# The low 64 columns of B: from ten split passes over the whole array to four full passes on its halves

## The chip, the cores and the metric

The kernel runs on one core of a Trainium2 chip. The metric is the device time of one execution in microseconds. The engines of the core are TensorE (PE, with its weight loads shown apart as PEld), VectorE (DVE), ScalarE (ACT), GpSimd (POOL) and SyncE (SP), each with its own stream of instructions, held in step by semaphores.

## The reference, cut to what matters

A small language-model tower over 32 sequences of 256 tokens and width D = 192: four gated recurrent layers, then one attention block and one quantised feed-forward block. The change touches one product in the layers:

```
def _block(x, g, bt, Wi, bi, cw, cb, wd, bd_, wB, bB_, wC, bC_, wo, bo):
    h = _layernorm(x, g, bt)
    uv = h @ Wi.T + bi
    u, v = (uv[..., :D], uv[..., D:])
    uc = _dwconv_causal(u, cw, cb)
    delta = jax.nn.softplus(uc @ wd.T + bd_)
    Bm = uc @ wB.T + bB_
    Cm = uc @ wC.T + bC_
    y = _selective_scan(uc, delta, Bm, Cm)     # decay exp(-delta), input uc * Bm, output sum(h * Cm)
    y = y * jax.nn.sigmoid(v)
    return x + (y @ wo.T + bo)
for l in range(4):
    x = _block(x, ...)
```

## The kernel before, in words

The rows of x stay in SBUF. In the layers the work is cut into items: one item is two sequences (2 x 256 tokens) of one layer, so 16 items a layer and 64 in all. Activations lie with the features on the partitions: the high 128 of the 192 features on 128 partitions (`uc_h`, both sequences side by side, 512 columns), the low 64 features of sequence 0 on partitions 0 to 63 and of sequence 1 on partitions 64 to 127 (`uc_l`, 256 columns).

Most products run on fp32r operands, which TensorE takes in one pass but which are rounded. To keep fp32 accuracy, the rows and the weights are split into a rounded part and a rest: ACT rounds `uc` into `ucr_h` and `ucr_l` (round_uc, L1031), DVE subtracts (rest_of_uc, L1299) into `ucr_r` and into the other half of `ucr_l`. ACT rounds the layer's weights `raw_z` into `w_z` (round_weights, L947) and DVE writes `w_z_rest` (split_weights, L1220). A product of 128 output columns is then five passes of 512 columns (z_product, L589). B's low 64 output columns are made by b_low_product (L598): for each of the two sequences five passes of 256 columns, and in each pass a 128-wide slice of `w_z` of which one half is zeros (`B_LOW`, the padding of `Z_COLS`), so that sequence 0 lands on PSUM partitions 0 to 63 of bank B_BL and sequence 1 on partitions 64 to 127. That is 10 of the passes of an item; the others of the z and C family are 20 of 512 columns, and uv_product has 15.

A product on plain fp32 operands shows in the trace as two records for each matmul instruction, one on fp32r as one. Plain fp32 is used in rows (L651): `w_o` with `sv_h` (L676, 128 rows of the array), and `w_o` with `sv_l` (L683) on the two halves of the array's rows, tile by tile in turn, half b writing bank `B_O[b]`. In the attention phase, values (L763) places four heads on the four quarters of the array's columns (L775); all four write one bank.

Each engine's order is written out by hand: steps (L254) runs one software-pipelined step for each item. On PE a step is uv of one item, z_c of the item before it, transposes, rows of the item two back, then b_c: z_product for B's high columns (bank B_BH), b_low_product (B_BL), z_product for C's (B_CH). b_c ends with semaphores `b_done` and `c_done`; DVE's recurrence (L1313) waits for them. Four early steps of layers 0, 1 and 2 (each layer's items 2 to 5) also carry the preparation of the next layer's weights: means (L566) on PE, centre_weights and split_weights on DVE, round_weights on ACT. The steps of the first layer carry DVE's place (L1230), which adds the position rows to the gathered embeddings.

Of the kernel before, what the change touches and what calls it, by code (L numbers as in the profile page):

```python
# [7 lines left out]
F32 = mybir.dt.float32  # L8
# [4 lines left out]
ACT = mybir.ActivationFunctionType  # L13
AX = mybir.AxisListType.X

P = 128
D = 192
HI, LO = 128, 64
S = 256
# [4 lines left out]

UV_H, UV_L, UV_V, UV_COLS = 0, 128, 256, 384

Z_H, Z_LC, B_PAD, B_H, C_H, Z_COLS = 0, 128, 256, 448, 576, 704

B_LOW = (B_PAD + 64, B_PAD)
EPS = 1e-5  # L30
H, DH = 12, 16
R = 4
# [4 lines left out]
F32R = mybir.dt.float32r  # L37
# [3 lines left out]
def wait(eng, sem, value):  # L41

    if isinstance(value, int) and value <= 0:
        return
    eng.wait_ge(sem, value)


def build(nc, tokens, embedding, pos_enc, w_uv_d, w_z_d, w_o_d, gain_d, vec_d, bout, w_qkv_d, b_qkv_d, w_out_d,
# [9 lines left out]
    with ExitStack() as ctx:  # L58
# [6 lines left out]
        def sem(name):  # L65
            return ctx.enter_context(nc.semaphore(name))
# [30 lines left out]
        def sa(name, shape, dt=F32):  # L97
            return layers_memory.enter_context(nc.sbuf_tensor(name, shape, dt))
# [4 lines left out]
        raw_z = sa("raw_z", [P, 2, Z_COLS])  # L103
# [3 lines left out]

        xs = sa("xs", [P, CT, 2 * D], F32R)
        ht = [sa(f"ht_{k}", [P, 2 * S], F32R) for k in range(3)]
        w_z = sa("w_z", [P, 2, 2, Z_COLS], F32R)  # L110
        w_z_rest = sa("w_z_rest", [P, 2, 2, Z_COLS], F32R)
        ucr_h = sa("ucr_h", [P, 2, 2 * S], F32R)

        ucr_l = sa("ucr_l", [P, 2, 2 * S], F32R)
        ucr_r = sa("ucr_r", [P, 2, 2 * S], F32R)
        w_o = sa("w_o", [P, L, 2, D])

        stats = sa("stats", [P, CT, 6])
        mv = sa("mv", [P, CT, 2])
# [6 lines left out]
        uc_h = sa("uc_h", [P, 2, 2, S])  # L126
        uc_l = sa("uc_l", [P, 2, S])
# [70 lines left out]
        w_rounded = sem("w_rounded")  # L198
# [48 lines left out]
        def half(b):  # L247

            return slice(b * LO, (b + 1) * LO)
# [309 lines left out]
        def _(pe):  # L559
# [38 lines left out]
            def b_low_product(l, s, out):  # L598


                for b in range(2):
                    c, w_s, q = slice(B_LOW[b], B_LOW[b] + HI), l % 2, slice(b * S, (b + 1) * S)
                    passes = ((w_z[:, w_s, 0, c], ucr_h), (w_z[:, w_s, 1, c], ucr_l), (w_z[:, w_s, 0, c], ucr_r),
                              (w_z_rest[:, w_s, 0, c], ucr_h), (w_z_rest[:, w_s, 1, c], ucr_l))
                    for k, (w, r) in enumerate(passes):
                        last = nc.tensor.matmul(out[:, 0:S], w, r[:, s, q], start=(b == 0 and k == 0),  # L606
                                                stop=(b == 1 and k == len(passes) - 1))
                return last

            def uv(it, centred):  # L610
# [79 lines left out]
            def b_c(it):  # L690
                if it is None:
                    return
                n, l, c, s = it
                wait(pe, ht_ready, ahead(n, 3))
                z_product(l, B_H, s, B_BH)
                b_low_product(l, s, B_BL).then_inc(b_done, 1)
                z_product(l, C_H, s, B_CH).then_inc(c_done, 1)
# [242 lines left out]
        def _(act):  # L940
# [6 lines left out]
            def round_weights(l):  # L947
                s = l % 2
                wait(act, c_done, (l - 1) * NCH)
                act.wait_ge(s_layer[l], W_LAYER)  # L950
                for k in range(2):
                    act.activation(w_z[:, s, k, :], raw_z[:, k, :], ACT.Identity).then_inc(w_rounded, 1)
                act.wait_ge(w_centred, 3 * (l + 1))
                for k in range(3):
                    act.activation(w_uv[:, s, k, :], raw_uv[:, k, :], ACT.Identity).then_inc(w_rounded, 1)
# [88 lines left out]
            def gates(it):  # L1044
# [9 lines left out]
                act.activation(sv_h[:, s, :], B_VH[:], ACT.Sigmoid, bias=v(l, 0, V_BV)).then_inc(sv_ready, 1)  # L1054

            round_weights(0)

            def turned(src, dst, t_sem, n, done):
# [58 lines left out]
            def step(at, l, k):  # L1117
                save_u(at(2), 1)
                first_tap(at(2), 1)
                save_u(at(2), 0)  # L1120
                first_tap(at(2), 0)
                decay(at(3))
                save_turned(at(1))
                round_rows(at(0))
                round_uc(at(2))
                gates(at(2))
                if (to := prepared(l, k, PREP_ROUND)) is not None:
                    round_weights(to)
                if l == L and k == 0:
                    act.wait_ge(s_w2, W2_ALL)  # L1130
                    act.activation(w_ffn[:, 0, :], w_ffn_words[:, 0, :].bitcast(I8), ACT.Identity)
                    act.activation(w_ffn[0:LO, 1, :], w_ffn_words[0:LO, 1, :].bitcast(I8), ACT.Identity)
                    act.activation(identb[:], ident[:], ACT.Identity).then_inc(s_identb, 1)
                elif l == L and k == 2:
                    save_h1(seq(0))
                    act.wait_ge(s_const, 6)
                    high_parts(seq(0), 0)
                    high_parts(seq(0), 1)
# [32 lines left out]
        def _(dve):  # L1171
# [47 lines left out]

            def split_weights(l):  # L1220
                s = l % 2
                dve.wait_ge(w_rounded, 5 * (l + 1))
                for k in range(2):
                    nc.vector.tensor_tensor(w_z_rest[:, s, k, :], raw_z[:, k, :], w_z[:, s, k, :].bitcast(F32),
                                            ALU.subtract).then_inc(w_split, 1)
                for k in range(2):
                    nc.vector.tensor_tensor(w_uv_rest[:, s, k, :], raw_uv[:, k, :], w_uv[:, s, k, :].bitcast(F32),
                                            ALU.subtract).then_inc(w_split, 1)
# [142 lines left out]
            place(1, 1, 1)  # L1371
            centre_weights(0)
            split_weights(0)

            def norm_statistics(first, second):
# [111 lines left out]
            def step(at, l, k):  # L1487
# [33 lines left out]
                if (to := prepared(l, k, PREP_SPLIT)) is not None:  # L1521
                    split_weights(to)
# [112 lines left out]
```

## Time and profile before

| | us |
|---|---|
| median of 3 runs | 1655.63 |
| lowest, highest | 1651.02, 1657.86 |
| the profiled execution | 1659.81 |
| its span, first to last instruction | 1657.9 |
| mean granted TensorE clock in the span | 0.966 of full speed |

Up to about 980 us of the span the layers run, then the attention phase. Start times in the trace count from the start of the span. PE is the engine with the largest busy share.

### The profile page before, as it was taken

The numbers are of one execution on the slowest core, as the hardware profiler recorded it, in microseconds if no ns is written. First come the engines' busy times: TensorE is split into PE (matmuls) and PEld (weight loads), VectorE is DVE, ScalarE is ACT, GpSimd is POOL, SyncE is SP. The second block draws the span as 40 slices with busy tenths as digits, with TensorE's granted clock in tenths as the row PEclk, the third lists the DMA queues.
The fourth block names the chain that finished last, engine by engine and source line by source line (L and its number), as shares of the span: only waits on it lengthen the run. The fifth ranks groups of instructions, "written<-read, shape, count | busy, mean of one in ns | idle before, by whom it ended". The sixth has DMA issues, their size and how long they took to land.

```text
span 1657.9 us, 36360 instructions
## 1 busy us (share of the span) xinstructions
PE 1555.3 (94%) x11137; PEld 1229.3 (74%) x11137; DVE 1365.5 (82%) x3414; ACT 1238.9 (75%) x2875; POOL 747.5 (45%) x1354
## 2 busy tenths in 40 slices
PE   3699999999999999999999988999999999999985
PEld 2578788878888888888888875666666666666653
DVE  4699999889999899999999875678888878888864
ACT  2587788688888778888888844677777777777763
POOL 6656633223333233333333244555565555555542
PEclk9799999999999999999999995999999999999997
DMA  7121100000000000000000000000000000000000
GB/s 165 31 59 28 23 8 1 1 33 0 0 1 1 1 1 0 0 1 1 1 0 0 1 1 1 2 7 11 11 10 15 10 10 10 10 10 10 15 12 25
DMA packets 16397, 21.98 MB, mean 13 GB/s; under 512 B 2928, under 2 KB 13808, under 8 KB 16304
## 3 DMA queue, kind: packets, MB, share of 16 engines
q1 hardware_dynamic: 13232, 14.54, 2.7%
q0 software_dynamic: 3072, 6.30, 2.4%
q8 instruction: 47, 0.77, 0.2%
q14 instruction: 46, 0.38, 0.1%
HBM read 14.14 MB, written 6.29 MB: 12 GB/s over the span
## 4 chain that ended last, share of the span: by engine, by line
PE 62%; ACT 14%; DVE 12%; issue 9%; POOL 1%; DMA 1%; DVEq 1%; ACTq 0%; POOLq 0%
PE bank L595 9%; PE bank L586 7%; PE bank L775 5%; PE bank L732 4%; PE bank L746 4%; PE bank L718 4%; PE bank L759 4%; PE bank L711 3%; PE bank L721 3%; PE bank L712 3%; PE bank L676 3%; ACT xs L1028 2%; DVE x L1360 2%; ACT ht L1018 2%; PE bank L606 2%
## 5 line engine op out<-in xcount | busy, mean ns | idle before, releaser
L1071 ACT ACTIVATE probs<-bank 128x512 f32<-128x512 f32 x384 | 207.1, 591 | 133.8 <-PE bank L759 131.0
L1406 DVE TENSOR_REDUCE mx<-bank 128x2 f32<-128x512 f32 x384 | 246.1, 682 | 26.6 <-PE bank L746 25.0
L441 POOL TENSOR_TENSOR x<-x,bo_row 128x768 f32<-128x768 f32 (+1 forms) x64 | 118.9, 1858 | 188.0 <-DVE ucr_r L1305 188.0
L586 PE MATMUL bank<-ht,w_uv 128*128 128x512 f32 x576 | 171.0, 407 | 16.5 <-ACT sv_l L1051 11.5
L759 PE MATMUL bank<-q_t,k_t 64*128 64x256 f32 x768 | 157.2, 353 | 8.7 <-ACT probs L1071 5.5
L417 POOL TENSOR_TENSOR lnt<-mv,const 128x4 f32<-128x4 f32 x64 | 20.5, 321 | 311.9 <-DVE mv L1270 311.8
L746 PE MATMUL bank<-k_t,q_t 64*128 64x256 f32 x768 | 141.2, 325 | 6.2 <-ACT k_t L1082 3.1
L1296 DVE SCALAR_TENSOR_TENSOR uc_h<-u_h,vec,uc_h 128x512 f32<-128x512 f32 x192 | 143.9, 750 | 2.9 <-ACT uc_h L989 2.9
L586 PEld LDWEIGHTS bank<-ht,w_uv 128*128 128x128 f32 x576 | 111.2, 196 | 46.3 <-issue 16.6
L1279 DVE SCALAR_TENSOR_TENSOR xs<-x,rstd,xs 128x192 fp32r<-128x192 f32 x256 | 90.0, 413 | 59.4 <-ACT xs L1028 59.4
L759 PEld LDWEIGHTS bank<-q_t,k_t 64*128 64x128 f32 x768 | 103.0, 188 | 39.7 <-issue 21.3
L499 POOL TENSOR_TENSOR parts<-qk_rows,parts 128x192 fp32r<-128x192 f32 x128 | 77.8, 628 | 99.9 <-ACT parts L1092 99.8
L586 PE MATMUL bank<-ht,w_uv_rest 128*128 128x512 f32 x384 | 122.0, 400 | 0.0
L968 ACT ACTIVATE u_l<-bank,vec 64x256 f32<-64x256 f32 x128 | 60.0, 469 | 78.1 <-PE bank L586 77.3
L985 ACT ACTIVATE uc_l<-bank,vec 64x256 f32<-64x256 f32 x128 | 71.9, 561 | 60.9 <-DVE inp_l L1322 59.9
L595 PE MATMUL bank<-ucr_h,w_z 128*128 128x512 f32 x256 | 107.5, 420 | 5.6 <-ACT ht L1018 5.4
L746 PEld LDWEIGHTS bank<-k_t,q_t 64*128 64x128 f32 x768 | 99.1, 194 | 16.0 <-ACT k_t L1082 9.1
L732 PE MATMUL bank<-identr,parts 128*128 128x128 f32 x768 | 105.9, 263 | 2.2 <-issue 2.1
L1081 ACT ACTIVATE q_t<-bank 128x256 fp32r<-128x256 f32 x192 | 73.5, 383 | 45.0 <-PE bank L732 44.9
L775 PE MATMUL bank<-probs,v_aug 128*32 128x256 f32 x1536 | 104.5, 390 | 0.2 <-issue 0.2
L1018 ACT ACTIVATE ht<-bank 128x512 fp32r<-128x512 f32 x192 | 100.8, 598 | 4.8 <-PE bank L647 3.3
L647 PE MATMUL bank<-identr,xs 128*128 128x128 f32 x768 | 76.2, 247 | 29.1 <-DVE xs L1279 18.3
(178 smaller groups left out, 4668.9 us busy)
## 6 DMA issues: line engine op xcount, KB each, us to landing
out_dram<-y_out SPq DMA_DIRECT2D x32, 192.0 KB, 2.0
raw_z<-w_z_dram SPq DMA_DIRECT2D x4, 704.0 KB, 5.3
raw_uv<-w_uv_dram SPq DMA_DIRECT2D x4, 576.0 KB, 3.9
emb<-embedding_dram,idx POOLq DMA_INDIRECT x64, 3.6
q_t<-mx_t SPq DMA_DIRECT2D x64, 6.0 KB
w_o<-w_o_dram SPq DMA_DIRECT2D x1, 768.0 KB, 5.4
bo_row<-bout_dram SPq DMA_DIRECT2D x4, 96.0 KB, 6.6
w_qkv<-w_qkv_dram SPq DMA_DIRECT2D x1, 288.0 KB, 7.1
```

What stands on the lines that cost most here:

```text
L441: nc.gpsimd.tensor_tensor(rows, rows, bo_row[:, l, :][:, None, :].broadcast_to([P, CT, D]), ALU.add).then_inc(x_biased, 1)
L586: last = nc.tensor.matmul(out[:], w, r[:], start=(k == 0), stop=(k == len(passes) - 1))
L595: last = nc.tensor.matmul(out[:], w, r[:, b, :], start=(k == 0), stop=(k == len(passes) - 1))
L732: last = nc.tensor.transpose(B_HEADS[g][:, (2 * o + t) * P:(2 * o + t + 1) * P].bitcast(F32R), parts[:, s, t, o, 2 * g:2 * g + 2, :].rearr ...
L746: last = nc.tensor.matmul(B_S[j][:, t * S:(t + 1) * S], q_t[q, s, g, t * P:(t + 1) * P], k_t[q, s, g, :], start=True, stop=True)
L759: last = nc.tensor.matmul(B_ST[j][:, t * S:(t + 1) * S], k_t[q, s, g, t * P:(t + 1) * P], q_t[q, s, g, :], start=True, stop=True)
L775: last = nc.tensor.matmul(bank[32 * h:32 * h + 32, c:c + S], v_aug[:, s, t, 4 * p + h, :], probs[:, (s + p) % 2, h // 2, (2 * (h % 2) + t) ...
L1018: last = act.activation(ht[g][:], B_T[g][:], ACT.Identity)
L1071: last = act.activation(probs[:, (s + g // 2) % 2, g % 2, 2 * j * S:2 * (j + 1) * S], B_ST[j][:], ACT.Exp, scale=float(DH) ** -0.5)
L1279: last = nc.vector.scalar_tensor_tensor(out=xs[:, k, D:2 * D], in0=x[:, tile_of(c, k)], scalar=rstd[:, s, k:k + 1], in1=xs[:, k, 0:D].bitc ...
L1296: nc.vector.scalar_tensor_tensor(out=uc, in0=uk, scalar=v(l, part, V_W0 + k), in1=uc, op0=ALU.mult, op1=ALU.add).then_inc(taps, 1)
L1406: last = nc.vector.tensor_reduce(mx[:, s, :, j * H // 2 + g], B_S[j][:].rearrange("p (t k) -> p t k", t=2), AX, ALU.max)
```

## The change

`b_low_product` takes four fp32 matmuls in place of ten fp32r passes. The high 128 input rows go through `w_b[:, l % 2, 0, :]` (128 x 64) and the unrounded `uc_h`, sequence 0 on the array's columns 0 to 63 and sequence 1 on columns 64 to 127; then the low 64 input rows through `w_b[half(b), l % 2, 1, :]` (64 x 64) and `uc_l`, sequence b on the rows and on the columns of half b. All four write bank B_BL, as before on partitions 0 to 63 and 64 to 127. `w_b` is a plain fp32 copy of B's low columns, written by ACT in round_weights beside `w_z`. The zero padding is gone: `w_z`, `w_z_rest` shrink from 704 to 512 columns and `raw_z` from 704 to 576, with the DMA that fills it. `w_rounded` counts 6 a layer in place of 5.

```diff
-Z_H, Z_LC, B_PAD, B_H, C_H, Z_COLS = 0, 128, 256, 448, 576, 704
-
-B_LOW = (B_PAD + 64, B_PAD)
+Z_H, Z_LC, B_H, C_H, B_L, Z_COLS = 0, 128, 256, 384, 512, 576
...
-        w_z = sa("w_z", [P, 2, 2, Z_COLS], F32R)
-        w_z_rest = sa("w_z_rest", [P, 2, 2, Z_COLS], F32R)
+        w_z = sa("w_z", [P, 2, 2, B_L], F32R)
+        w_z_rest = sa("w_z_rest", [P, 2, 2, B_L], F32R)
...
+        w_b = sa("w_b", [P, 2, 2, LO])
...
                 for b in range(2):
-                    c, w_s, q = slice(B_LOW[b], B_LOW[b] + HI), l % 2, slice(b * S, (b + 1) * S)
-                    passes = ((w_z[:, w_s, 0, c], ucr_h), (w_z[:, w_s, 1, c], ucr_l), (w_z[:, w_s, 0, c], ucr_r),
-                              (w_z_rest[:, w_s, 0, c], ucr_h), (w_z_rest[:, w_s, 1, c], ucr_l))
-                    for k, (w, r) in enumerate(passes):
-                        last = nc.tensor.matmul(out[:, 0:S], w, r[:, s, q], start=(b == 0 and k == 0),
-                                                stop=(b == 1 and k == len(passes) - 1))
+                    nc.tensor.matmul(out[half(b), 0:S], w_b[:, l % 2, 0, :], uc_h[:, s, b, :], start=True, stop=False,
+                                     skip_group_check=True)
+                for b in range(2):
+                    last = nc.tensor.matmul(out[half(b), 0:S], w_b[half(b), l % 2, 1, :], uc_l[half(b), s], start=False,
+                                            stop=True, skip_group_check=True)
...
                 for k in range(2):
-                    act.activation(w_z[:, s, k, :], raw_z[:, k, :], ACT.Identity).then_inc(w_rounded, 1)
+                    act.activation(w_z[:, s, k, :], raw_z[:, k, 0:B_L], ACT.Identity).then_inc(w_rounded, 1)
+                act.activation(w_b[:, s], raw_z[:, :, B_L:Z_COLS], ACT.Identity).then_inc(w_rounded, 1)
...
-                dve.wait_ge(w_rounded, 5 * (l + 1))
+                dve.wait_ge(w_rounded, 6 * (l + 1))
                 for k in range(2):
-                    nc.vector.tensor_tensor(w_z_rest[:, s, k, :], raw_z[:, k, :], w_z[:, s, k, :].bitcast(F32),
+                    nc.vector.tensor_tensor(w_z_rest[:, s, k, :], raw_z[:, k, 0:B_L], w_z[:, s, k, :].bitcast(F32),
                                             ALU.subtract).then_inc(w_split, 1)
...
-    z = columns(mats, (("z", 1), ("z", 0), ("C", 0), ("0", 0), ("B", 0), ("0", 0), ("B", 1), ("C", 1)))
+    z = columns(mats, (("z", 1), ("z", 0), ("C", 0), ("B", 1), ("C", 1), ("B", 0)))
```

PE inside b_c, before: the last pass of B's high columns (bank5) and sequence 0's five passes into bank6 (B_BL). The same five rows stand there once more for sequence 1, and then C's product into bank7.

```order
L595 MATMUL bank5<-ucr_l,w_z_rest 128x512
L606 MATMUL bank6<-ucr_h,w_z 128x256
L606 MATMUL bank6<-ucr_l,w_z 128x256
L606 MATMUL bank6<-ucr_r,w_z 128x256
L606 MATMUL bank6<-ucr_h,w_z_rest 128x256
L606 MATMUL bank6<-ucr_l,w_z_rest 128x256
```

The same place on PE after the change; L602 is the product over the high input rows, L605 that over the low ones.

```order
L595 MATMUL bank5<-ucr_l,w_z_rest 128x512
L602 MATMUL bank6<-uc_h,w_b 64x256 x2
L605 MATMUL bank6<-uc_l,w_b 64x256 x2
L595 MATMUL bank7<-ucr_h,w_z 128x512
L595 MATMUL bank7<-ucr_l,w_z 128x512
```

Ten instructions have become four between the same neighbours; nothing else on PE has moved.

ACT in the first steps of a layer, where the gates' sigmoids (L1051, L1054) are followed by the rounding of the next layer's weights.

```order
 L1051 ACTIVATE sv_l<-bank,vec 64x256 x2
 L1054 ACTIVATE sv_h<-bank,vec 128x512
-L952 ACTIVATE w_z<-raw_z 128x704 x2
+L951 ACTIVATE w_z<-raw_z 128x512 x2
+L952 ACTIVATE w_b<-raw_z 128x128
 L955 ACTIVATE w_uv<-raw_uv 128x384 x3
```

Two long instructions are shorter by 192 columns each, and one of 128 columns has come behind them.

DVE in the first steps of a layer, between an item's residual (L1360) and the next step.

```order
 L1305 TENSOR_TENSOR ucr_r<-uc_h,ucr_h 128x512
 L1360 SCALAR_TENSOR_TENSOR x<-bank,ysb,x 128x192 x4
-L1224 TENSOR_TENSOR w_z_rest<-raw_z,w_z 128x704 x2
+L1224 TENSOR_TENSOR w_z_rest<-raw_z,w_z 128x512 x2
 L1227 TENSOR_TENSOR w_uv_rest<-raw_uv,w_uv 128x384 x2
```

Only the width of the two subtractions is other.

## Rows read from the trace of the kernel before

**Rows 1.** Busy time by stretches of the span, the columns in the first row.

```profile
core 0: us, PE busy (x) PEld busy (x) DVE busy (x) ACT busy (x) POOL busy (x), PEclk, DMA share, GB/s
100.00:237.00 137.00, 126.38 (x789) 107.80 (x788) 129.12 (x316) 105.46 (x216) 74.50 (x107) 1.00 0.15 31
242.00:306.00 64.00, 64.00 (x409) 56.69 (x407) 60.14 (x159) 54.10 (x109) 21.14 (x35) 1.00 0.00 1
374.00:538.00 164.00, 164.00 (x1068) 145.96 (x1067) 152.93 (x407) 140.99 (x286) 56.61 (x96) 1.00 0.00 1
605.00:947.00 342.00, 342.00 (x2224) 304.69 (x2224) 316.47 (x840) 296.50 (x601) 115.21 (x193) 1.00 0.00 1
990.00:1045.00 55.00, 49.39 (x210) 31.09 (x210) 26.84 (x57) 20.49 (x60) 23.96 (x53) 0.52 0.00 1
```

**Rows 2.** The chain of waits, one step of layer 2: start, us, engine, line; lines left out are PE.

```profile
699.91 0.98 PE bank L647 x12
...
704.23 1.36 PE bank L595 x5
705.59 1.18 PE bank L606 x10
706.77 1.16 PE bank L595 x5
...
713.60 0.98 PE bank L647 x12
```

**Rows 3.** The chain of waits, within one step of layer 0.

```profile
156.82 1.56 DVE x L1235
```

**Rows 4.** PE in order of time, the same step: start, us, instruction.

```profile
702.97 0.92 PE L683 MATMUL bank<-w_o,sv_l 64*128 64x192 f32 x8
...
704.16 0.50 PE L595 MATMUL bank<-ucr_h,w_z 128*128 128x512 f32 x1
704.50 0.39 PE L595 MATMUL bank<-ucr_l,w_z 128*128 128x512 f32 x1
704.73 0.40 PE L595 MATMUL bank<-ucr_r,w_z 128*128 128x512 f32 x1
...
705.42 0.28 PE L606 MATMUL bank<-ucr_h,w_z 128*128 128x256 f32 x1
...
706.61 0.40 PE L595 MATMUL bank<-ucr_h,w_z 128*128 128x512 f32 x1
```

**Rows 5.** PE in order of time, attention phase, from four very short stretches.

```profile
1153.75 0.24 PE L732 MATMUL bank<-identr,parts 128*128 128x128 f32 x1
1153.93 0.62 PE L775 MATMUL bank<-probs,v_aug 128*32 128x256 f32 x5
1154.17 0.59 PE L775 MATMUL bank<-probs,v_aug 128*32 128x256 f32 x5
1154.60 0.40 PE L775 MATMUL bank<-probs,v_aug 128*32 128x256 f32 x4
1154.93 0.59 PE L711 MATMUL bank<-w_qkv,h_t 128*128 128x384 f32 x1
```

**Rows 6.** Groups by line and shape: busy us, mean ns of one.

```profile
L775 PEld LDWEIGHTS bank<-probs,v_aug 128*32 128x32 f32 x1536 | 40.5, 110 | 25.0 <-issue 2.2
L706 PEld LDWEIGHTS bank<-ident,xn 128*64 128x64 f32 x64 | 7.3, 115 | 0.1
L1224 DVE TENSOR_TENSOR w_z_rest<-raw_z,w_z 128x704 fp32r<-128x704 f32 x8 | 8.6, 1121 | 0.6 <-ACT w_uv L955 0.6
L1305 DVE TENSOR_TENSOR ucr_r<-uc_h,ucr_h 128x512 fp32r<-128x512 f32 x64 | 44.3, 692 | 0.9
L952 ACT ACTIVATE w_z<-raw_z 128x704 fp32r<-128x704 f32 x8 | 5.9, 781 | 6.5 <-DMA raw_z<-w_z_dram 6.5
L1041 ACT ACTIVATE ucr_h<-uc_h 128x512 fp32r<-128x512 f32 x64 | 40.5, 633 | 1.6
```

**Rows 7.** The chain of waits, where layer 3's weights are prepared.

```profile
582.48 2.23 DVE w_z_rest L1224 x2
```

More of the change, by code:

```diff
@@ L1605 @@
     uv = _np.stack([uv[:HI], _np.concatenate([uv[HI:], uv[:LO]], axis=0), uv[LO:]], axis=2)
-    mats["0"] = _np.zeros_like(mats["B"])
-    z = columns(mats, (("z", 1), ("z", 0), ("C", 0), ("0", 0), ("B", 0), ("0", 0), ("B", 1), ("C", 1)))
+    z = columns(mats, (("z", 1), ("z", 0), ("C", 0), ("B", 1), ("C", 1), ("B", 0)))
     z = _np.stack([z[:HI], _np.concatenate([z[HI:], z[HI:]], axis=0)], axis=2)
```

## The prediction, made before the changed kernel was run

> **What bounds the kernel now.** I read the busy time by stretches first. From 242 to 306, 374 to 538 and 605 to 947 us PE is busy for the whole stretch, 64 + 164 + 342 = 570 us, while DVE is at 60.14 of 64, 152.93 of 164 and 316.47 of 342, and the granted clock is at its full level [rows 1]. Then the chain of waits: in such a stretch it is made of PE pieces alone, and one step of the loop, an item of 16 a layer, takes 713.60 - 699.91 = 13.69 us [rows 2]. What lengthens or shortens PE's work there moves the end by just as much. 570 / 13.69 = 41.6 steps are of this kind; about 3 more lie among the first steps of layers 1 and 2, partly on PE, so I count 45. In layer 0 it is otherwise: from 100 to 237 us DVE is busy 129.12 of 137 us and PE 126.38 [rows 1], and the chain runs through ACT and DVE, with DVE's place at 1.56 us on it [rows 3]. PE has some 10.6 / 137, or 8% of a step, about 1.2 us, to spare there, and a few tenths more or less on PE cost nothing. That cover is gone as soon as PE's addition to a step passes 1.2 us.
>
> **What goes away.** Ten passes of 256 columns: they start at 705.42 and C's first pass at 706.61, so 1.19 us [rows 4]; the chain has 1.18 for them [rows 2]. That is 0.12 us a pass, since the weights of each are loaded while the one before streams. The split rows and their rests are still needed for the other products, so nothing goes on ACT or DVE inside a step.
>
> **What comes.** Four fp32 matmuls, eight records, in two pairs. Whether the two of a pair run side by side is the first question. The nearest row is L775: fp32, 256 columns, 128 rows of the array, four tiles in different columns and one PSUM bank. Each short stretch shows four records of one start and the first of the next; the starts are 1153.93, 1154.17, two more rounds up to 1154.60, and the next product at 1154.93 [rows 5]. So tiles side by side in the columns do run together, a round of records takes (1154.60 - 1154.17) / 2 = 0.215 us, the first 0.24 and the last, up to the next product, 0.33. Two rounds, a first and a last, are 0.57. The tiles are now 64 wide; a load of 64 columns shows a mean of 115 ns against 110 for 32 [rows 6], so I add 0.01: 0.58 for the high pair, and the same for the low pair.
>
> The second question is the way in and out. The last 128-wide transpose starts at 1153.75 and the first L775 at 1153.93 [rows 5], 0.18 us, where a transpose takes 0.98 / 12 = 0.08 in its row [rows 2]: leaving the whole array costs 0.10. After L683 and L686, which use half the array's rows, the first whole-array pass takes 704.50 - 704.16 = 0.34 us against 704.73 - 704.50 = 0.23 for the next [rows 4]: its weights could not be loaded ahead, and coming back costs 0.11. The chain's pieces say the same in one number: five passes behind such a change take 1.36 us and five without one 1.16 [rows 2].
>
> Sum a step: 0.10 + 0.58 + 0.58 + 0.11 = 1.37 us in place of 1.19, so **+0.18 us**. The gain in streaming, 4 x 0.215 = 0.86 against 1.19, is more than eaten by three changes of the array's shape.
>
> No row shows the middle change, from 128 rows x 64 columns to 64 x 64. If it cost nothing, the first pair's last round would be 0.215 and not 0.33, and the step +0.06. At the other end, each pair could pay the first-pass price of a 128-wide load, 0.11 and not the 0.025 of the 32-wide one in the 0.24: +0.34 with both. I take +0.18, since every change that the rows do show is paid, and keep both ends. The skill has a rule for the middle change: the Trainium skill, TensorEngine Tiling (Array Packing), Key Properties, says that changing the tiling mode, not just the tile, drains TensorE. No row here shows this pair of shapes; by the rule the sum stays at +0.18, without it it would be +0.06.
>
> Over 45 steps: +8.1 us, with +2.7 and +15.3 as the ends.
>
> **The weights.** DVE's two subtractions of a layer shrink from 704 to 512 columns. Where layer 3's weights are prepared, early in layer 2, the chain holds 2.23 us of them [rows 7]; scaled by 512 / 704 that is 1.62, 0.6 less. By the means, 1121 ns at 704 and 692 for a subtraction of 512 [rows 6], it is 2 x 0.43 less, and scaling 692 up to 704 (951) gives 2 x 0.26. I take 0.4 us at each of the three preparations, **-1.2 us** in all. ACT: two of 781 ns become two of about 633, the nearest of 512 columns [rows 6], and one of 128 columns, which costs something between nothing and 633: from -0.30 to +0.34 us each time, and I take nothing. ACT queues the w_uv rounding behind it, and DVE's split waits for that, so at the upper end 1.0 us comes back over the three. The smaller transfer of raw_z starts a layer ahead of its use, and in layer 0 the gathered rows come later than it: nothing. The new read of `uc_h` and `uc_l` by PE adds no wait: DVE's use of B's product already stands between it and the next write to them. `b_done` and `c_done` come 0.18 us later, with only recurrence behind them, which in the PE-bound steps waits on neither.
>
> **Sum.** +8.1 - 1.2 = +6.9 us. On the profiled execution, 1659.81 us with a span of 1657.9, that gives 1666.7; it lies 4.2 us, 0.25%, over the median of 1655.63, and on the median it gives 1662.5.
>
> **Rivals.** (A) The forecast, 1655.63 + 1.5 to + 14.1: 1657 to 1670.
>
> (B) Slower: the low pair does not run side by side. Its two tiles lie in different halves of the array's rows and write one bank. In this kernel the row halves of L683 write two banks, and L775's four tiles share a bank but stand in the same rows; nothing in the trace has different rows and one bank. If they take turns, two more rounds of 0.215 are added, 0.43 us a step, and 45 x (0.18 + 0.43) - 1.2 = +26.3: 1682. It decides from the first item on. Against it: the two also lie in different columns, so they write different partitions. The Trainium skill, TensorEngine Tiling (Array Packing), Gotcha 1 (PSUM Pressure), says that different row tiles cannot access the same PSUM bank simultaneously; that rule names rows alone and would give this rival, and no row here tests it. 12%.
>
> (C) Neither pair overlaps: four more rounds, 45 x (0.18 + 0.86) - 1.2 = +45.6: 1701. Against it stands L775 [rows 5]. 5%.
>
> (D) Faster: tiles 64 wide are changed into and out of for less than these rows show, so that the middle change and the way in are free and only 4 x 0.215 + 0.03 + 0.11 = 1.00 us stands for the 1.19. Then 45 x -0.19 - 1.2 = -9.8: 1646. Against it: the way in of L775 has its 0.10. 8%.
>
> (E) The clock. From 990 to 1045 us, entering the attention phase, it is at 0.52 of full, almost all at the lower level (1.2 GHz), with PE busy 49.39 of 55 [rows 1]. If the new timing lets it rise at the start of this stretch, up to half of those PE-bound 49 us, 25 us, come back; a second such stretch would cost as much. Nothing in the change reaches there, so 3% for each.
>
> **How the numbers follow.** A has 65%, B 12, C 5, D 8, E 6, other mishaps 4, split 1 faster and 3 slower. A measurement of this kernel tells about 0.5%, 8.3 us, from no change. A's centre, +6.9, lies near that bound: I put 42 of its 65 within and 23 beyond. Faster: D 8 + E 3 + 1 = 12%. Slower: A 23 + B 12 + C 5 + E 3 + 3 = 46%, and I round A's share down by 2 for the unsure 45 steps: 44%. Within 0.5%: 44%. The range takes in A, B and D, 1646 to 1683, 85% of the chance; what it leaves out is C and E.
>
> **What would show it.** In the profile after, L602 and L605: two records starting within some 0.01 us of each other and pairs 0.215 to 0.25 apart for side by side; records one after the other 0.215 apart mean B or C. From the last L595 of B's high product to C's second pass: 1.65 us before in the row's starts (0.23 + 1.19 + 0.23), 1.83 by the forecast. Between L602's last start and L605's first 0.33 if the middle change is paid, 0.22 if not. A step of 13.87 us in the chain, still made of PE alone; in layer 0 steps as long as before. One w_z_rest near 0.7 us. The forecast is wrong if steps elsewhere than in b_c change, or if the low-clock stretch behind 990 us moves or grows.

## The result and the profile after

| | before | after |
|---|---|---|
| median, us | 1652.42 (12 runs) | 1667.76 (12 runs) |
| lowest, highest | 1650.99, 1661.10 | 1662.85, 1671.50 |
| the profiled execution | 1659.81 | 1669.41 |
| its span | 1657.9 | 1667.6 |

The ratio after to before is 1.0081, 95% interval 1.0066 to 1.0095: the change makes the kernel slower by 0.8%. All ratios compare fast runs alone, which leaves out one of e6's twelve, at 1888.89 us and a mean clock of 0.74.

The chain of waits of the changed kernel, one step of layer 2 from one item's L675 to the next (L675 is the old L676, L682 the old L683; start, us, engine, line, count):

```profile
706.04 1.37 PE bank L675 x8
...
709.39 1.36 PE bank L595 x5
710.75 0.58 PE bank L602 x4
711.33 0.58 PE bank L605 x4
711.91 1.36 PE bank L595 x5
713.26 3.42 PE bank L586 x15
...
719.94 1.37 PE bank L675 x8
```

The step is 719.94 - 706.04 = 13.90 us, where it was 13.69 [rows 2], and it is still made of PE alone. L602 and L605 together take 1.16 us in place of L606's 1.18, so the product itself has become a trifle cheaper. But C's five passes behind it now take 1.36 us and not 1.16, the price that B's five passes behind the row halves had paid before.

PE's own records in order of time, the same step (start, us, instruction), from a few short stretches; each line merges neighbours of one kind:

```profile
710.35 0.40 PE L595 MATMUL bank<-ucr_l,w_z_rest 128*128 128x512 f32 x1
710.67 0.65 PE L602 MATMUL bank<-uc_h,w_b 128*64 128x256 f32 x4
710.94 0.39 PE L602 MATMUL bank<-uc_h,w_b 128*64 128x256 f32 x2
711.26 0.65 PE L605 MATMUL bank<-uc_l,w_b 64*64 64x256 f32 x4
711.52 0.38 PE L605 MATMUL bank<-uc_l,w_b 64*64 64x256 f32 x2
711.84 0.50 PE L595 MATMUL bank<-ucr_h,w_z 128*128 128x512 f32 x1
712.17 0.40 PE L595 MATMUL bank<-ucr_l,w_z 128*128 128x512 f32 x1
712.41 0.40 PE L595 MATMUL bank<-ucr_r,w_z 128*128 128x512 f32 x1
```

Four records of L602 start at 710.67 (two) and 710.94 (two), four of L605 at 711.26 and 711.52. So both pairs run side by side. Between the last round of one shape and the first of the next lie 711.26 - 710.94 = 0.32 and 711.84 - 711.52 = 0.32 us, where a round inside such a group takes 0.215 [rows 5]. The last pass of B's high product lasts 710.67 - 710.35 = 0.32 until L602 starts, where 0.23 is usual, and C's first pass 712.17 - 711.84 = 0.33, its neighbour 0.24. The weight loads show what is different; these are PEld's rows, each with the time without a load ahead of it in brackets ("issue": it waited for nothing that the profile shows):

```profile
710.67 0.20 PEld L602 LDWEIGHTS bank<-uc_h,w_b 128*64 128x64 f32 x4 [0.36 <-issue]
711.26 0.20 PEld L605 LDWEIGHTS bank<-uc_l,w_b 64*64 64x64 f32 x4 [0.39 <-issue]
711.84 0.19 PEld L595 LDWEIGHTS bank<-ucr_h,w_z 128*128 128x128 f32 x1 [0.38 <-issue]
```

Each time the shape changes, the first load starts together with its own matmul and not one matmul ahead, after 0.36 to 0.39 us without any load.

Here is a trap for whoever reads busy times. The first row is of the kernel before, one of five alike, the other two of the changed one (busy us, mean ns of one):

```profile
L606 PE MATMUL bank<-ucr_h,w_z 128*128 128x256 f32 x128 | 36.2, 283 | 0.0
```

```profile
L602 PE MATMUL bank<-uc_h,w_b 128*64 128x256 f32 x256 | 42.2, 409 | 0.0
L605 PE MATMUL bank<-uc_l,w_b 64*64 64x256 f32 x256 | 42.0, 406 | 0.0
```

Five groups of 36 us each, 181 us, have become 84 us, and the kernel is slower. A record is longer than the distance to the next start (0.28 against 0.12 us for L606 in [rows 4] and the chain), so neighbouring records overlap, and five groups that take turns count the same time more than once. Only starts add up: by the chain's pieces it is 64 x 1.18 = 76 us before and 64 x 1.16 = 74 us after.

The stretches that answer to [rows 1], with the same columns (us, PE, PEld, DVE, ACT, POOL busy, clock, DMA share, GB/s), and 306 to 374 us, which stands for the preparation of layer 2's weights:

```profile
100.00:237.00 137.00, 129.44 (x775) 102.05 (x773) 129.13 (x316) 105.80 (x217) 74.19 (x106) 0.99 0.14 30
306.00:374.00 68.00, 65.85 (x349) 51.38 (x348) 57.05 (x151) 48.77 (x101) 18.29 (x32) 0.87 0.05 18
605.00:947.00 342.00, 342.00 (x2152) 279.26 (x2150) 312.20 (x829) 294.57 (x594) 110.60 (x192) 1.00 0.00 1
990.00:1045.00 55.00, 45.91 (x199) 31.75 (x197) 29.01 (x59) 18.40 (x58) 25.95 (x51) 0.55 0.00 1
```

In layer 0 PE's busy time goes from 126.38 to 129.44 us of 137 while DVE's stays, 129.12 and 129.13: the addition sinks into PE's spare time there. From 605 to 947 us PE has no idle time in either kernel. In the same time DVE gets through 829 instructions where it had 840, ACT through 594 where it had 601: fewer steps fit in.

At the preparation of the weights (duration in ns, smallest, median, largest):

```profile
L1224 DVE TENSOR_TENSOR w_z_rest<-raw_z,w_z x8: 678/686/1319, 22.5 to 588.6; 128x512 fp32r<-128x512 f32 x8
```

and ACT's two forms:

```profile
L951 ACT ACTIVATE w_z<-raw_z 128x512 fp32r<-128x512 f32 x8 | 4.6, 621 | 6.4 <-DMA raw_z<-w_z_dram 6.4
L952 ACT ACTIVATE w_b<-raw_z 128x128 f32<-128x128 f32 x4 | 1.2, 296 | 0.0
```

**Where the time went.** Of the 63 intervals from one item's first L676 (L675) to the next, 44 lie at 13.7 us before and at 13.90 after. Two of them lie among the preparations of weights. The other 42 are 8.5 us longer together, 0.18 us each in layer 1 and 0.20 to 0.21 behind it. The four intervals in which layer 2's weights are prepared last 69.9 us and lasted 67.4, the four with layer 3's 66.7 and 66.8. The last three, where the attention phase begins, are 0.4 us longer, and what stands behind the last item's first L675 is 0.5 us longer. At the front the first L675 starts 1.4 us earlier and the ten intervals behind it are 0.5 us shorter together. 8.5 + 2.5 - 0.2 + 0.4 + 0.5 - 1.4 - 0.5 = 9.8 us, which is the difference of the spans but for rounding.

Layer 2's +2.5 us comes from one interval: it lasts 18.55 us where it lasted 14.50, and the other three are 1.6 us shorter. In it the granted clock is at its lower level (1.2 GHz) for 10 us, with PE busy throughout. e1's trace of the same kernel has this interval at 18.57 us and the same stretch one microsecond earlier. The first row is of the changed kernel, the second of e1, with the columns of [rows 1]; from 357 to 367 us of the kernel before the clock is at 1.00.

```profile
357.00:367.00 10.00, 10.00 (x44) 7.67 (x43) 8.42 (x26) 7.66 (x17) 4.41 (x8) 0.51 0.03 13
356.00:366.00 10.00, 10.00 (x44) 7.61 (x42) 8.36 (x25) 7.59 (x17) 4.47 (x8) 0.50 0.03 12
```

### The profile page after: what moved, and what is told of

The parts are those of the page before. It is cut to its first block, busy times and chain, and to the rows that moved or that the text cites. A ratio compares the mean times of both kernels' runs of the same rounds, so it can differ in the third digit from the quotient of the medians.

```text
span 1667.6 us, 36108 instructions
## 1 busy us (share of the span) xinstructions
PE 1570.8 (94%) x11009; PEld 1176.5 (71%) x11009; DVE 1364.1 (82%) x3414; ACT 1240.0 (74%) x2879; POOL 740.6 (44%) x1354
## 4 chain that ended last, share of the span: by engine, by line
PE 77%; ACT 8%; DVE 6%; issue 6%; POOL 1%; DMA 1%; DVEq 0%; ACTq 0%; POOLq 0%
PE bank L595 15%; PE bank L586 11%; PE bank L774 5%; PE bank L731 4%; PE bank L745 4%; PE bank L675 4%; PE bank L758 4%; PE bank L717 4%; PE bank L710 3%; PE bank L720 3%; PE bank L711 3%; PE bank L646 3%; PE bank L682 2%; PE bank L679 2%; PE bank L815 2%
## 5 line engine op out<-in xcount | busy, mean ns | idle before, releaser
L595 PE MATMUL bank<-ucr_h,w_z 128*128 128x512 f32 x256 | 114.6, 448 | 4.6 <-ACT ht L1018 4.6
L1028 ACT ACTIVATE xs<-x,rstd 128x192 fp32r<-128x192 f32 (+1 forms) x256 | 95.7, 444 | 8.3 <-POOL rstd L429 6.7
```

The source lines that it names most:

```text
L595: last = nc.tensor.matmul(out[:], w, r[:, b, :], start=(k == 0), stop=(k == len(passes) - 1))
L1028: last = act.activation(xs[:, k, 0:D], x[:, tile_of(c, k)], ACT.Identity, scale=rstd[:, s, k:k + 1])
```

## The experiments

The theory: the price is the change of the array's shape (rows x columns of a tile), of which the change adds three to a step, in 44 to 48 steps that PE bounds. The rivals: the fp32 products are slow in themselves, wherever and in whatever shape they stand; the pairs gain nothing from running side by side; or far more steps, or fewer, are bound by PE.

### e1, the changed kernel again

No edit.

> The changed kernel once more, for a second trace and beside the others on the same chip. Theory (three changes of the array's shape a step, paid in the PE-bound steps): steady step 13.90 us as in the first trace of after, ratio 1.006 to 1.010. The clock's low stretches among the first steps of layers 1 and 2 may lie elsewhere and move the total by 2 to 5 us; the steady step must not move.

Measured: median 1668.09 us, ratio 1.0070 (1.0048 to 1.0092). Steady step 13.90 us again. Step and ratio agree with the first measurement; the two intervals overlap from 1.0066 to 1.0092.

### e2, the four matmuls ahead of B's high product

```diff
-                z_product(l, B_H, s, B_BH)
-                b_low_product(l, s, B_BL).then_inc(b_done, 1)
+                b_low_product(l, s, B_BL)
+                z_product(l, B_H, s, B_BH).then_inc(b_done, 1)
```

Inside b_low_product the low pair comes first, and the wait for `ht_ready` stands ahead of the last loop of rows.

> The same four matmuls, but placed right behind the row-half products of rows and ahead of B's high product, low pair first, so that the array's shape is changed three times between rows and C's product (64x128 to 64x64 to 128x64 to whole) where the changed kernel has four. The wait for the turned rows stands ahead of the last products of rows. Shape-change theory: B's last pass loses its 0.09 us and C's first its 0.10, steady step 13.90 - 0.19 = 13.71 us, time within 0.3% of before. Rival (the fp32 products are slower in themselves, wherever they stand): step stays at 13.90, ratio 1.008.

Measured: median 1655.99 us, ratio to before 1.0001 (0.9985 to 1.0017). Its chain of waits (L605 is the low pair's line here as L602 is the first pair's; both are 0.58):

```profile
704.52 0.85 PE bank L682 x8
705.37 0.34 PE bank L687 x7
705.71 0.58 PE bank L602 x4
706.29 0.58 PE bank L605 x4
706.87 2.51 PE bank L595 x10
709.39 3.40 PE bank L586 x15
```

The same four matmuls take the same 1.16 us, and the ten passes of B and C behind them 2.51 us, where the changed kernel needs 1.36 + 1.36 = 2.72. The step is 715.06 (L646) - 701.38 = 13.68 us by the chain; the expected 13.71 holds, and the rival that the products are slow wherever they stand falls, as it wanted 13.90. What the place saves is one change of shape, since rows has already left the whole array.

### e3, no change of shape at all

```diff
-                for b in range(2):
-                    nc.tensor.matmul(out[half(b), 0:S], w_b[:, l % 2, 0, :], uc_h[:, s, b, :], start=True, stop=False,
-                                     skip_group_check=True)
-                for b in range(2):
-                    last = nc.tensor.matmul(out[half(b), 0:S], w_b[half(b), l % 2, 1, :], uc_l[half(b), s], start=False,
-                                            stop=True, skip_group_check=True)
+                for b in range(2):
+                    nc.tensor.matmul(out[:, 0:S], w_bh[:, l % 2, (1 - b) * LO:(1 - b) * LO + HI], uc_h[:, s, b, :],
+                                     start=(b == 0), stop=False)
+                last = nc.tensor.matmul(out[:, 0:S], w_bl[:, l % 2, :], uc_l[:, s], start=False, stop=True)
```

`w_bh` holds the high weights between two blocks of zeros, `w_bl` the low weights twice on a diagonal.

> No change of shape at all: the high rows as two fp32 matmuls of 128 weight columns, half of them zeros, and both low products as one fp32 matmul with block-diagonal weights. Six records one after the other instead of four rounds of two. Shape-change theory: 6 x 0.215 = 1.29 us for the product in place of 1.18 before, nothing lost at its neighbours, step 13.80 us, total 3 to 5 us under the changed kernel although half as much again is streamed. Rival (streamed fp32 columns are what costs): two rounds more, step 13.90 + 0.43 = 14.33, 20 us over the changed kernel.

Measured: median 1663.96 us, ratio to before 1.0048 (1.0027 to 1.0068). The chain:

```profile
707.31 1.36 PE bank L596 x5
708.67 0.86 PE bank L603 x4
709.53 0.43 PE bank L605 x2
709.97 1.15 PE bank L596 x5
711.12 3.42 PE bank L587 x15
```

Six records one after the other, 0.86 + 0.43 = 1.29 us as expected, and C's five passes are back at 1.15. The step is 717.79 (L674) - 703.97 = 13.82. With two rounds more to stream, this is 4.1 us faster by the medians than the changed kernel on the same chip. The ratios' intervals of e3 and e1 overlap, so the 4.1 us alone prove little; the step decides, 13.82 us where the rival wanted 14.33. Streamed columns are not what made the changed kernel slow. e3 also answers a rival that was not named: in the changed kernel the operands go from fp32r to fp32 and back at the same places as the shape changes. Here they still do, and nothing is lost: from the first start of B's five passes to the next product's lie 1.267 us (1.266 before, 1.360 in the changed kernel).

### e4, the kernel before with four passes more

```diff
                     for k, (w, r) in enumerate(passes):
+                        for _ in range(4 if b == 0 and k == 0 else 0):
+                            nc.tensor.matmul(out[:, 0:S], w, r[:, s, q], start=True, stop=True, skip_group_check=True)
                         last = nc.tensor.matmul(out[:, 0:S], w, r[:, s, q], start=(b == 0 and k == 0),
```

> The kernel before with four more passes of 256 columns ahead of each item's product with B's low columns (the first pass repeated, each time as a new start). It measures how many of the 64 steps PE bounds: 4 x 0.118 = 0.47 us a step. Theory (42 to 45 steps, layer 0 has over 1 us of cover): +20 to +21 us, layer 0's steps stay at 15.2 us. Rival (all 64 steps pay): +30 us.

Measured: median 1677.16 us, ratio 1.0140 (1.0113 to 1.0168), which is +23.2 us (18.7 to 27.8).

```profile
715.38 0.47 PE bank L607 x4
715.85 1.19 PE bank L608 x10
```

The added passes take 0.47 us and the step is 14.17, 0.48 more. 23.2 / 0.48 = 48 steps (39 to 58) pay. The 45 of the prediction lies in it, all 64 don't. The trace counts them without the clock's part in the time: 44 of its 63 intervals are 14.17 to 14.19 us long, and layer 0's steps stay at 15.2 us. 48 x 0.21 = 10.1 us is then what this measure gives for the changed kernel, 44 x 0.21 = 9.2 by the count. The interval of the first measurement, 10.9 to 15.7 us, lies above both, that of e1, 7.9 to 15.2, around them.

### e5, the low pair in the high pair's shape

```diff
-                    last = nc.tensor.matmul(out[half(b), 0:S], w_b[half(b), l % 2, 1, :], uc_l[half(b), s], start=False,
+                    last = nc.tensor.matmul(out[half(b), 0:S], w_bl[:, l % 2, b, :], uc_l[:, s], start=False,
```

In `w_bl` the 64 rows of the other sequence are zeros; `w_b` keeps the high rows' weights alone.

> The changed kernel with the low pair in the high pair's shape: the 64 rows of each sequence's low weights stand in a 128-row weight tile whose other rows are zeros, so that all four matmuls are 128 rows x 64 columns and the middle change of shape is gone. Same place as in the changed kernel, still four rounds. Shape-change theory: the emptying (0.10) and the exposed load (0.05) in the middle go, step 13.90 - 0.15 = 13.75 us, total 6 to 7 us under the changed kernel, ratio to before 1.002 to 1.004. Rival (the middle change costs nothing by itself, the low pair is only slow): step 13.90.

Measured: median 1656.47 us, ratio to before 0.9998 (0.9978 to 1.0018).

```profile
707.97 1.36 PE bank L596 x5
709.33 0.58 PE bank L603 x4
709.91 0.43 PE bank L606 x4
710.35 1.35 PE bank L596 x5
```

The low pair goes from 0.58 to 0.43 us, two rounds of 0.215 with nothing between, and the step to 718.37 (L676) - 704.63 = 13.74. The middle change alone costs 0.15 us, and padding with zeros is the cheaper way. The pairs' columns of the array still alternate here at no price: it is the change of shape that costs, not that of place.

The time missed its expectation, a ratio of 1.002 to 1.004: it is lower, 0.9998 with 1.0018 as its upper end. e5 to e7 ran on another chip than e1 to e4, where the kernel before has a median of 1659.12 us and the changed kernel was not measured, and the granted clocks of the compared runs differ. Point 8 below takes this out as far as the runs allow, and leaves +1.6 us (1.001) for e5.

### e6, the same ahead of B's high product

The edits of e5 and of e2 together, with the high pair first.

> The same in the place of e2_low_first, right behind the row-half products and ahead of B's high product: one change of shape more in a step than in the kernel before, where the changed kernel has two more than this. Shape-change theory: e2's step of 13.67 less 0.15 = 13.52 us, and 45 to 48 PE-bound steps x -0.17 give 7 to 8 us under before, ratio 0.995; DVE's 12.7 us of work a step still fits in. Rival (below some 13.6 us the step is bound by the round through ACT and DVE): step stays at 13.6 or above and the time within 0.2% of before.

Measured: median 1652.66 us, ratio to before 0.9967 (0.9948 to 0.9987): 0.3% faster than the kernel before on the same chip; the expected 0.995 lies in the interval.

```profile
702.73 0.58 PE bank L603 x4
703.31 0.43 PE bank L606 x4
703.74 2.51 PE bank L596 x10
706.25 3.50 PE bank L587 x15
```

The product and its neighbours cost what the theory says, 0.58 + 0.43 and 2.51. But the 15 passes of uv take 3.50 us and no longer 3.40, and the step from L676 to L676 is some 13.6 us, most between 13.6 and 13.7, where 13.52 was expected. The time that PEld waited from 630 to 920 us, in us, times and the longest:

```profile
PEld bank L587 <- issue: 3.5, 15, 0.3
PEld bank L587 <- ACT sv_l L1058: 1.1, 6, 0.2
```

The profile puts 1.1 of these 4.6 us down to ACT's gates, which clear uv's bank, and for the rest names nobody. But in every step from 605 to 940 us uv's first load starts 50 or 113 ns behind the end of the last gate on `sv_l`, where in the changed kernel that distance is 380 ns. So PE now comes to uv before ACT has cleared the bank. The rival, that the round through the other engines begins to bind at some 13.6 us, holds for the step. The time does not decide: it is 0.33% under before, but the upper end of the interval, 0.9987, lies within the rival's 0.2%. How much of the 0.1 us is ACT's was not tried.

### e7, the high pair one after the other

```diff
-                    nc.tensor.matmul(out[half(b), 0:S], w_b[:, l % 2, 0, :], uc_h[:, s, b, :], start=True, stop=False,
-                                     skip_group_check=True)
+                    nc.tensor.matmul(out[half(0), b * S:(b + 1) * S], w_b[:, l % 2, 0, :], uc_h[:, s, b, :], start=True,
+                                     stop=False, skip_group_check=True)
```

> Leaves B's product with the high input rows of sequence 1 in another place of the bank than it belongs: both sequences' high products go through the same half of the array's columns, one after the other; shapes, counts and changes of shape are those of the changed kernel. It prices the overlap alone: two rounds of 0.215 more, step 13.90 + 0.43 = 14.33 us, some 20 us over the changed kernel. If the step stays at 13.90, the pair did not gain from running side by side.

Measured in one execution: 1681.93 us, some 14 us over the changed kernel's two medians, of which e1's is from another chip.

```profile
714.59 1.01 PE bank L602 x4
715.60 0.58 PE bank L605 x4
...
717.53 3.40 PE bank L586 x15
```

L602 takes 1.01 us where it took 0.58: side by side the pair saves 0.43 us, two rounds. The step is 14.30, not 14.33, since uv is at 3.40 here and not at 3.42. The total is some 6 us less than expected, and the trace shows where: the four intervals with layer 2's weights last 64.5 us and not 69.9, those with layer 3's 64.2 and not 66.7. The changed kernel's interval of 18.55 us is 14.61 here, with no 10 us at the low clock in it.

## Why the prediction was right, and where it was short

The forecast was a time of 1662.5 us, the measured one is 1667.8. The likeliest case, three paid changes of shape, is the one that happened, and its range, 1657 to 1670, holds the time. Of the chances, the one that came true is slower by over 0.5%. The mechanism is shown. That the time is only 5 us off is in part luck: the base was 3.2 us too high. From the later median of 1652.42 the same sum gives 1659.3, 8.5 us short, and the range of that case would have ended at 1666.5, below what was measured.

1. **PE bounds the steady steps, by starts and chain.** Right: 13.69 to 13.90 us with PE busy throughout, and layer 0 took its share into its slack. e4 gives 48 paying steps by the time, 39 to 58, and 44 by the trace, against 45.
2. **Ten passes cost 1.19 us.** Right, and they are worth 0.12 each (e4).
3. **Pairs run side by side, 0.58 us each.** Right: 0.58 and 0.58 in the chain. e7 prices it: 0.43 us a pair. Rivals B and C fall at once. The low pair, different rows and different columns and one bank, does run side by side: two records at 711.26 and two at 711.52. The Trainium skill, TensorEngine Tiling (Array Packing), Gotcha 1 (PSUM Pressure), says that different row tiles cannot access the same bank at the same time; this pair, whose tiles differ in columns too, shows no sign of it, and the measurement decides.
4. **In 0.10 and back 0.11 us.** Measured 0.09 and 0.10: B's five passes 1.266 to 1.360 us from first start to the next line's, as the median of 22 and more steps, C's 1.161 to 1.263.
5. **The middle change is paid.** Right, against rival D and the lower end: e5 takes it away and gains 0.15 us a step. Here the rule of the Trainium skill, TensorEngine Tiling (Array Packing), Key Properties, that a change of the tiling mode drains TensorE, agrees with the trace for a pair of shapes that no row of before showed.
6. **The sum a step was 0.03 short,** +0.18 forecast and +0.21 measured. The term that was missing is outside b_c: the 15 passes of uv go from 3.40 to 3.42 us by the chain. In e1, e3 and e5 they are at 3.42 too, in e2, e4 and e7 at 3.40. No order of instructions on PE tells these apart; that they meet something of another engine is an argument only, and it stays open. Over 45 steps the 0.03 us are 1.3 us.
7. **The weights' 1.2 us.** DVE's subtraction went from a mean of 1121 to a median of 686 ns, at 512 columns; its means are 1121 and 920, 0.2 us apart, so 0.4 us a preparation as taken. ACT's sum is 2 x 621 + 296 = 1538 ns against 1562, nothing, as taken. At the end the saving can't be told from other shifts: the four intervals with layer 3's weights are 0.2 us shorter in spite of PE's additions, and three of the four with layer 2's 1.6 us, but the fourth is 4.05 us longer, in the low clock. That the added changes of shape bring the clock down there was not tested. A long interval of this kind also stands in e2's trace among layer 3's preparation (18.41 us) and in e5's and e6's in layer 0 (19.47 and 19.35 us), and at these three places the intervals of before, e3, e4 and e7 are at most 16.0 us.
8. **The base and the clock.** The sum left the clock out. +6.9 us was forecast; between the two spans lie +9.7, and the ratio of 1.0081 is +13.4 us (10.9 to 15.7), e1's +11.6. The runs differ in their mean granted clock. Of the 18 runs of before beside e1, 11 are at 0.969 or more of full; of the changed kernel's 18, here and in e1, none is above 0.968. A straight line of time against clock through these runs of e1 to e4's chip, one slope for all kernels, gives 1.0 us for each 0.001 of clock, and at equal clock the changed kernel is 8.1 us slower than before, e4 21.5 us. These are estimates, worked out from the runs' times and clocks. 21.5 / 0.48 = 45 steps, the number of the prediction, and 45 x 0.21 - 1.2 = 8.2 us is the changed kernel's. On the other chip e5 comes out 1.6 us slower than before and e6 6.0 us faster. So of e1's +11.6 us some 8 are what the change costs at a given clock, and some 3.5 go along with a lower clock. The +13.4 us of the first measurement can't be parted this way, as the clocks of its runs of before are not on record, but its 12 runs of the changed kernel lie on the same line. Whether the change is what lowers the clock is not shown.
9. **Rival E, the clock behind the layers,** did not come: from 990 to 1045 us it is at 0.55 of full where it was at 0.52. That it can come is seen in e4's trace. There the clock is at 0.50 for 23 and for 13 us with 11 us near full between them, where before it is at 0.50 for 54 us on end, and the part behind the last item's first w_o product takes 669.2 us, where it took 675.5.

The chance of 44% for within 0.5% was given by a centre that lay 1.4 us under the bound of 8.3. The missing 0.03 us a step brings it nearly to the bound, and the clock's share is enough to move it over.

## What to carry to other kernels

Count changes of the array's shape as a cost of their own, beside streamed columns and passes: each here costs some 0.15 to 0.2 us, as much as one to two fp32r passes of 256 columns. Put products of one shape next to each other, and pad a small one with zeros to its neighbour's shape before giving it a shape of its own (e5, e6). Read such a product's price from starts, never from the busy sums of its lines. When an effect is below 1%, compare runs of the same granted clock before reading a ratio.

## What the runs showed of the hardware

- A change between 128 x 128, 128 x 64 and 64 x 64 tiles costs 0.09 to 0.10 us in the last matmul ahead of it (0.32 us until the next start, where it is 0.23 or 0.215 without a change). The first matmul behind it costs 0.10 us more when it loads 128 columns (0.33 against 0.23), and 0.05 when 64 (0.27 against 0.215). Coming back from 64 x 128 tiles shows the same 0.11 us behind [rows 4].
- The two records of an fp32 matmul don't hold up the next matmul in another tile: of the four records of L602, two start at 710.67 and two at 710.94. The trace does not name a record's tile; that each two are one of each sequence is inferred from e7, where both matmuls use one tile and the four take 1.01 us and not 0.58.
- Tiles in different rows and different columns that write one bank run side by side, 0.58 us for four records like the pair in the same rows.
- The granted clock can fall to its lower level for 10 us with PE busy all the while: 10.00 of 10 us from 357 to 367 us of the changed kernel, at 0.51 of full. In the 34 us before it PE was busy 32.48 us, and its wait of 1.52 us ended at 356.20. The interval with this stretch lasts 18.55 us and without it 14.50.
